# Causal attention with its score products in two row halves of the array, as 32-bit parts

## The reference

```
xn = layernorm(x)                                   # 4 sequences of 1024 tokens, 256 wide
Q, K, V = heads(xn @ W_q.T), heads(xn @ W_k.T), heads(xn @ W_v.T)     # 16 heads of 16
scores = Q @ K.T * 16 ** -0.5;  scores[k > q] = -inf
s = merge(softmax(scores) @ V) @ W_o.T
g = silu(two_layer_local_attention_network(xn))
out = x + s * g
```

## Time and profile before

| | |
|---|---|
| median of 3 runs | 2184.76 us (2183.27 to 2184.91) |
| profiled execution | 2185.67 us, span 2183.9 us |
| TensorE, busy | 1980.0 us (91%), weight loads 1414.1 us |
| VectorE, busy | 1559.4 us (71%) |
| ScalarE, busy | 1110.6 us (51%) |
| GpSimd, busy | 1072.4 us (49%) |
| mean granted clock of TensorE | 0.946 of 2.4 GHz |
| maxima products L517 | 768, 241.2 us busy |
| mask products L520 | 512 |
| maxima reductions L650 | 768, 375.9 us busy |
| score products L544 | 768, 191.8 us busy |
| weighted sums L562 | 1536 records (two for each of 768 products), 165.5 us busy |
| exponentials L627 | 384, 300.3 us busy |

### The profile page before, as it was taken

The page is one execution under the profiler, slowest core; times in us unless marked ns, Lnnn a source line. Parts: engine busy times, 40 slices in busy tenths (PEclk is TensorE's granted clock), DMA queues, the critical chain, the costliest instruction groups (busy, mean ns, idle before and its releaser), DMA issues. The chain is left out here.

```text
span 2183.9 us, 43787 instructions
## 1 busy us (share of the span) xinstructions
PE 1980.0 (91%) x13824; PEld 1414.1 (65%) x13888; DVE 1559.4 (71%) x2744; ACT 1110.6 (51%) x2339; POOL 1072.4 (49%) x903
## 2 busy tenths in 40 slices
PE   5869999999996899999997999779999999699976
PEld 4633334343432688888875888668888888578875
DVE  5657878778872799999995443269999999654324
ACT  3405656565665566666664222156666666422213
POOL 3431212112222666666663877476666666287730
PEclk9869999999998899999998999889999999799988
DMA  6892465464531000000022111200000002211137
GB/s 210 273 198 34 68 88 70 65 88 65 70 50 63 13 24 24 24 24 24 24 64 60 30 58 58 86 9 25 22 24 24 24 24 68 62 29 58 49 111 240
DMA packets 163938, 143.24 MB, mean 66 GB/s; under 512 B 30327, under 2 KB 144351, under 8 KB 163679
## 3 DMA queue, kind: packets, MB, share of 16 engines
q1 hardware_dynamic: 162462, 140.23, 27.4%
q10 hardware_dynamic: 1344, 1.31, 0.2%
HBM read 90.89 MB, written 50.35 MB: 65 GB/s over the span
## 5 line engine op out<-in xcount | busy, mean ns | idle before, releaser
L650 DVE TENSOR_REDUCE ca_mx<-ca_pR 128x1 f32<-128x512 f32 (+3 forms) x768 | 375.9, 549 | 91.0 <-PE ca_pR L520 47.8
L627 ACT ACTIVATE ca_pr<-ca_pS 128x1024 f32<-128x1024 f32 (+3 forms) x384 | 300.3, 813 | 244.2 <-PE ca_pS L544 185.0
L459 POOL TENSOR_SCALAR_AFFINE_SELECT ca_pr<-ca_pr 128x256 f32<-128x256 f32 x256 | 104.3, 408 | 430.3 <-ACT ca_pr L627 428.0
L879 ACT ACTIVATE w_pe<-w_pS,w_nmax 128x256 f32<-128x256 f32 x512 | 234.8, 484 | 142.3 <-DVE w_nmax L989 142.3
L802 POOL TENSOR_TENSOR w_tsn<-w_qk,w_tab 128x512 f32<-128x512 f32 x128 | 203.2, 1610 | 174.9 <-DVE w_pn L998 161.2
L517 PE MATMUL ca_pR<-ca_ks,ca_qs 96*128 96x512 bf16 (+3 forms) x768 | 241.2, 351 | 18.8 <-DVEq L703 16.2
L998 DVE TENSOR_SCALAR w_pn<-w_pe,w_rsum 128x256 f32<-128x256 f32 x512 | 227.3, 505 | 4.5
L544 PE MATMUL ca_pS<-ca_qs,ca_ks 98*128 98x512 bf16 (+3 forms) x768 | 191.8, 333 | 15.1 <-issue 13.2
L517 PEld LDWEIGHTS ca_pR<-ca_ks,ca_qs 96*128 96x128 bf16 x768 | 73.4, 99 | 186.5 <-DVE ca_mx L650 125.6
L810 POOL TENSOR_TENSOR w_rs<-w_ssc,mhalf 128x16 f32<-128x16 f32 x64 | 187.6, 2931 | 5.3
L1363 ACT ACTIVATE f_gl<-f_pH,f_b1g 128x512 f32<-128x512 f32 x96 | 66.2, 690 | 204.4 <-PE f_pH L1479 204.4
(11 more groups left out here) (163 smaller groups left out, 4777.3 us busy)
## 6 DMA issues: line engine op xcount, KB each, us to landing
QKP<-p_parts SPq DMA_DIRECT2D x32, 384.0 KB, 3.2
ca_qs<-QKP SPq DMA_DIRECT2D x96, 128.0 KB, 6.5
ca_ks<-QKP SPq DMA_DIRECT2D x96, 128.0 KB, 7.0
VA<-p_vaug SPq DMA_DIRECT2D x8, 1024.0 KB, 5.4
ca_va<-VA SPq DMA_DIRECT2D x16, 512.0 KB, 10.4
w_xt<-X SPq DMA_DIRECT2D x64, 128.0 KB, 2.0
X<-w_x SPq DMA_DIRECT2D x64, 128.0 KB, 1.7
f_hh<-X SPq DMA_DIRECT2D x32, 256.0 KB, 4.9
```

Of the source, the lines that this page charges most:

```text
L627: act.activation(pr[:, k % 2, pair, :, 0:w], pS[:, pair, :, 0:w], ACT.Exp, scale=CS).then_inc(p_ready, 1)
L650: dve.tensor_reduce(mx[:, i, h, ch:ch + 1], pR[jb % RING][:, 0:w], AX.X, ALU.max, negate=True).then_inc(ring_free, 1)
L879: ins = act.activation(pe_[:, h], pS[:, bank, slot], ACT.Exp, bias=nmax[:, n:n + 1], accum_out=sums[:, h:h + 1])
```

## The change

The queries and keys are kept as two 32-bit parts, high and low, where the high part is rounded to what a one-pass 32-bit product (`float32r`) takes. One ScalarE pass and one VectorE subtraction make them; the second ScalarE pass and GpSimd's subtraction go. A score needs three terms of 16 rows (high x high, high x low, low x high), 48 rows, and two more for the shift: 50. Two heads then lie in the two halves of the 128 rows, from partition 0 and from partition 64, and each half is multiplied by itself, into its own bank. The scores' two heads and the maxima's two heads are issued as such twos. A maxima pair waits for both of its banks before its first product, and the masks, still over 128 rows, follow both products. The jobs are reordered so that the two heads `r` of a pair `p` are neighbours, the plan of jobs per step changes to even numbers, the shift is placed by four transfers and the ones by six.

```diff
-PAIRS = [(0, 0), (0, 1), (0, 2), (1, 0), (1, 1), (2, 0)]
-SHIFT_ROW = len(PAIRS) * CD
-SROWS = SHIFT_ROW + 2
+TERMS = [(0, 0), (0, 1), (1, 0)]
+SHIFT_ROW = len(TERMS) * CD
+HALF_ROWS = 64
-LOADS = 2 * len(PAIRS) + 1
+LOADS = 2 * 2 * len(TERMS) + 1
...
-    parts = QKP[n].rearrange("(z h d) c s -> z c d h s", z=2, h=GH)
+    parts = QKP[n].rearrange("(z p r d) c s -> z c r d p s", z=2, p=2, r=2)
     out = []
-    for r, (a, k) in enumerate(PAIRS):
-        rows = slice(r * CD, (r + 1) * CD)
-        out += [(qs[rows, u], parts[0, a]), (ks[rows, u], parts[1, k])]
+    for r in range(2):
+        for t, (a, k) in enumerate(TERMS):
+            rows = slice(r * HALF_ROWS + t * CD, r * HALF_ROWS + (t + 1) * CD)
+            out += [(qs[rows, u].bitcast(F32), parts[0, a, r]), (ks[rows, u].bitcast(F32), parts[1, k, r])]
...
-        parts = sb("p1_parts", [P, CG, 3, SUP * P], BF16)
-        rest = sb("p1_rest", [P, CG, SUP * P], F32)
+        parts = sb("p1_parts", [P, CG, 2, SUP * P], F32R)
...
-                for g in range(CG):
-                    pool.wait_ge(part1, ONE + s * CG + g + 1)
-                    pool.tensor_tensor(parts[:, g, 2], rest[:, g], parts[:, g, 1],
-                                       ALU.subtract).then_inc(part2, 1)
...
-                    act.activation(parts[:, g, 0], pQ[:, g], ACT.Copy).then_inc(part0, 1)
-                    act.wait_ge(rest_ready, ONE + CG + u + 1)
-                    act.activation(parts[:, g, 1], rest[:, g], ACT.Copy).then_inc(part1, 1)
+                    act.activation(parts[:, g, 0], pQ[:, g], ACT.Copy).then_inc(part_hi, 1)
...
-                    dve.wait_ge(part0, ONE + u + 1)
-                    dve.wait_ge(part2, ONE + u + 1)
-                    dve.tensor_tensor(rest[:, g], pQ[:, g], parts[:, g, 0], ALU.subtract).then_inc(rest_ready, 1)
+                    dve.wait_ge(part_hi, ONE + u + 1)
+                    dve.tensor_tensor(parts[:, g, 1], pQ[:, g], parts[:, g, 0].bitcast(F32),
+                                      ALU.subtract).then_inc(part_lo, 1)
...
-    MAXJOBS = [(h, i, ch) for i in range(TPB - 1, -1, -1) for h in range(GH) for ch in range(1 + i // 4)]
+    MAXJOBS = [(p, r, i, ch) for i in range(TPB - 1, -1, -1) for p in range(2) for ch in range(1 + i // 4)
+               for r in range(2)]
-    PER = [6, 5, 4, 4, 5, 5, 5, 5, 2, 0, 0, 0]
-    EARLY = {10: (0, 3), 11: (3, 7)}
-    A, B = 2, 3
+    PER = [6, 4, 4, 4, 6, 6, 6, 4, 0, 0, 0, 0]
+    EARLY = {10: (0, 4), 11: (4, 8)}
+    A, B = 2, 4
...
-        shift = sb("ca_shift", [2 * GH, SEQ], BF16)
+        shift = sb("ca_shift", [2 * GH, SEQ], F32R)
+        one = sb("ca_one", [2, 2, SEQ], F32)
...
-            for u in range(SLOTS):
-                pool.memset(ks[SHIFT_ROW:SROWS, u, :, :], 1.0).then_inc(ones, 1)
-                pool.wait_ge(ones, ONE + u + 1)
+            pool.memset(one[:, :, :], 1.0).then_inc(made, 1)
...
                 for part in range(2):
-                    sp.dma_start(qs[SHIFT_ROW + part:SHIFT_ROW + part + 1, u, :, :],
-                                 shift[part * GH:(part + 1) * GH, :]).then_inc(shifted[u], 16)
+                    for r in range(2):
+                        row = r * HALF_ROWS + SHIFT_ROW + part
+                        sp.dma_start(qs[row:row + 1, u, :, :].bitcast(F32),
+                                     shift[part * GH + 2 * r:part * GH + 2 * r + 2, :].bitcast(F32)).then_inc(shifted[u], 16)
...
+                sp.wait_ge(made, ONE + 4)
+                for u in range(SLOTS):
+                    for r in range(2):
+                        row = r * HALF_ROWS + SHIFT_ROW
+                        sp.dma_start(ks[row:row + 2, u, :, :].bitcast(F32), one[:, :, :]).then_inc(ones, 16)
...
-                h, i, ch = MAXJOBS[idx]
-                k0 = ch * 512
-                w = min((i + 1) * P - k0, 512)
-                bank = ring(*job)
-                diag = k0 + w == (i + 1) * P
-                ins = pe.matmul(bank[:, 0:w], qs[0:SHIFT_ROW, u, h, i * P:(i + 1) * P],
-                                ks[0:SHIFT_ROW, u, h, k0:k0 + w], start=True, stop=not diag)
-                if diag:
-                    ins = pe.matmul(bank[:, w - P:w], K.identb[:, :], mask_q[:, :], start=False, stop=True)
-                ins.then_inc(ring_full, 1)
+                first, n_ring = job
+                banks = [ring(first + r, n_ring) for r in range(2)]
+                for r in range(2):
+                    p, half, i, ch = MAXJOBS[idx + r]
+                    rows = slice(r * HALF_ROWS, r * HALF_ROWS + SHIFT_ROW)
+                    k0 = ch * 512
+                    w = min((i + 1) * P - k0, 512)
+                    diag = k0 + w == (i + 1) * P
+                    ins = pe.matmul(banks[r][:, 0:w], qs[rows, u, p, i * P:(i + 1) * P], ks[rows, u, p, k0:k0 + w],
+                                    start=True, stop=not diag)
+                    if not diag:
+                        ins.then_inc(ring_full, 1)
+                for r in range(2):
+                    if diag:
+                        pe.matmul(banks[r][:, w - P:w], K.identb[:, :], mask_q[:, :], start=False, stop=True)\
+                          .then_inc(ring_full, 1)
...
-                for hh in range(2):
-                    h = pair * 2 + hh
-                    ins = pe.matmul(pS[:, pair, hh, 0:w], ks[:, u, h, j * P:(j + 1) * P],
-                                    qs[:, u, h, q0:q0 + w], start=True, stop=True)
+                for r in range(2):
+                    rows = slice(r * HALF_ROWS, r * HALF_ROWS + SHIFT_ROW + 2)
+                    ins = pe.matmul(pS[:, pair, r, 0:w], ks[rows, u, pair, j * P:(j + 1) * P],
+                                    qs[rows, u, pair, q0:q0 + w], start=True, stop=True)
```

More of the change, by code:

```diff
@@ L113, in phase_project @@
         t_ready, t_hi, t_lo = sem("p1_t_ready"), sem("p1_t_hi"), sem("p1_t_lo")
-        q_ready, part0, rest_ready, part1, part2 = (
-            sem("p1_q_ready"), sem("p1_part0"), sem("p1_rest_ready"), sem("p1_part1"), sem("p1_part2"))
+        q_ready, part_hi, part_lo = sem("p1_q_ready"), sem("p1_part_hi"), sem("p1_part_lo")
         part_stored = [sem(f"p1_part_stored{i}") for i in range(CG)]
@@ L148, in rest_of @@
                 for g in range(CG):
-                    sp.wait_ge(part2, ONE + CG + s * CG + g + 1)
+                    sp.wait_ge(part_lo, ONE + CG + s * CG + g + 1)
                     sp.dma_start(QKP[it * CG + g, :, :, j * 512:(j + 1) * 512],
-                                 parts[:, g]).then_inc(part_stored[g], 16)
+                                 parts[:, g].bitcast(F32)).then_inc(part_stored[g], 16)
                     if isinstance(s, int) and s == SUPERS - 2:
@@ L246, in _ @@
             start_at_one(dve, mine + K.stacks[3])
-            dve.sem_inc(rest_ready, CG)
+            dve.sem_inc(part_lo, CG)
             dve.sem_inc(v_copied, 2)
@@ L316, in step @@
                 for g in range(CG):
-                    pe.wait_ge(rest_ready, ONE + s * CG + g + 1)
+                    pe.wait_ge(part_lo, ONE + s * CG + g + 1)
                     ws = slice(g * P, (g + 1) * P)
@@ L574, in first @@
                 pe.wait_ge(loaded[0], ONE + LOADS * 16)
-                for idx in range(NJ):
+                for idx in range(0, NJ, 2):
                     maxima(idx, 0, 0, (idx, 0))
                 load_wait(1, 0)
-                for idx in range(NEARLY):
+                for idx in range(0, NEARLY, 2):
                     maxima(idx, 1, 1, (NJ + idx, 0))
@@ L586, in do @@
                     for job, kind, which in jobs:
+                        if kind in ("max", "early") and which % 2:
+                            continue
                         if kind == "max":
@@ L598, in step @@
                 if not started:
-                    pe.wait_ge(ones, ONE + SLOTS)
-                pe.wait_ge(shifted[u], ONE + (it + 1) * 2 * 16)
+                    pe.wait_ge(ones, ONE + SLOTS * 2 * 16)
+                pe.wait_ge(shifted[u], ONE + (it + 1) * 4 * 16)
                 for k in range(NSTEP):
@@ L645, in take_max @@
             def take_max(idx, job):
-                h, i, ch = MAXJOBS[idx]
+                p, r, i, ch = MAXJOBS[idx]
                 w = min((i + 1) * P - ch * 512, 512)
@@ L649, in take_max @@
                 dve.wait_ge(ring_full, ONE + n * RJ + jb + 1)
-                dve.tensor_reduce(mx[:, i, h, ch:ch + 1], pR[jb % RING][:, 0:w], AX.X, ALU.max,
+                dve.tensor_reduce(mx[:, i, 2 * r + p, ch:ch + 1], pR[jb % RING][:, 0:w], AX.X, ALU.max,
                                   negate=True).then_inc(ring_free, 1)
@@ L695, in step @@
                     elif kind == "shift":
-                        dve.wait_ge(shifted[u], ONE + (it + 1) * 2 * 16)
+                        dve.wait_ge(shifted[u], ONE + (it + 1) * 4 * 16)
                         take_shift((job, n))
@@ L1729, in program @@
         X = nc.dram_tensor("X", [(2 * LAYERS + 1) * ST_ROWS, D], F32, kind="Internal").ap()
```

(6 more changed lines are left out.)

1 line of the change is left out of this document (removed).

## The result

2375.51 us median (2357.55 to 2386.44, 4 runs) against 2184.84 us (2183.27 to 2186.38, 4 runs) before: a ratio of 1.086 [1.0804, 1.0917]. Forecast were 2229 us and a range up to 2290 us: slower was right, the size was not. The profiled execution took 2386.4 us where before took 2185.7, so the 200.7 us between these two have to be found. Three numbers of the timeline hold them: the first maxima product moved from 136.3 to 122.4 us (-13.9), from there to the first scores product it took 50.0 instead of 31.7 us (+18.3), and from the first to the last scores product, called the scores span from here on, 707.4 instead of 511.1 us (+196.3).

The account below looks back on a forecast made before the run. TensorE was taken to bind, VectorE close behind. Profiled 2185.7 us + 33 (15 iterations) + 11 (start of the block) = 2229.7, so a 2229 us median; own range 2205 to 2255, 8-in-10 range 2160 to 2290.

Parts of the forecast that it names:

- What binds, and the prices: Attention loop: TensorE binds with 29.4 us of work in 31.4, VectorE close behind; a 512-column pair in halves costs 0.23 us.
- rival 3: Scores and maxima: halves don't overlap for rounded 32-bit data, +8 us an iteration, 2315 us; chance 0.07.
- a masked pair: Maxima on the diagonal: a 512-column pair with masks and mode changes costs 0.70 us, where products and masks took 0.55.
- mode changes: Loop: TensorE's switches between row halves and full rows cost 8.4 us an iteration against 2.9 before, adding 5.5.
- rival 1: Loop: no drain between halves and mask, VectorE becomes the bound, 2168 us; chance 0.20 with every other way to a gain.
- The iteration: Loop, one head group: 33.6 us against 31.4 before, between 31.2 and 34.5; +33 us over 15 iterations.
- TensorE's own work: Loop, per iteration: products, masks, weighted sums, transposes and mode changes total 28.0 us against 29.4 before.
- The granted clock in the loop should stay near 1: Sign to check in the loop: TensorE's granted clock, 0.98 before, should stay near 1.
- rival 4: Loop: new waits drop the clock for a fifth of it, about +84 us more, 2290 to 2310 us; chance 0.10.
- The start of the block: First maxima before the first scores: 28 pairs worked out at 39.5 us against 27.1; +11 us taken, bounds 0 and +16.
- The projection: Before the attention block: splitting and moving the parts taken as 0, bounds -4 and +4 us.
- The shift's copy: Shift placement: 32-bit copy at most +1.4 us, four transfers +1.25; cost 0 in the loop, within +11 at the start.

Follow-up runs that it names:

- e13: Changed kernel with 14 more rows of zeros in each half (products of 62 and 64 rows): 2307.09 us, 1.0556 of before.
- e5: Kernel before (bf16, 96-row products, one-bank waits) with only the changed kernel's order and plan of jobs: 2204.98 us, 1.0092 of before.
- e4: Kernel before's bf16 96-row products with the changed kernel's order, plan and two-bank wait: 2272.6 us, 1.0392 of before.
- e11: Changed kernel with its two parts, stacks, shift and ones in bf16 instead of 32 bits (less exact): 2269.94 us, 1.0354 of before.
- e8: Changed kernel's 32-bit parts without halves, each head on full-array rows 0 to 66 (17 of zeros), in before's loop: 2438.35 us.
- e7: Changed kernel's 32-bit row halves, but each maxima product singly with its own half's mask and one bank, before's order and plan: 2283.07 us, 1.0437 of before.
- e15: e7 with the bf16 types of e11, leaving only the row halves of the loop's changes: 2199.8 us, 1.0049 of before.
- e1: Changed kernel with VectorE reducing only the last 128 columns of each maxima bank, so banks come free early: 2241.02 us, 1.0261 of before.
- e3: Changed kernel with every scores pair issued twice into the same banks: 2317.68 us, 1.0585 of before.
- the pairs in the table: Four pairs of kernels whose loops differ in rows of zeros alone: clock 0.66 to 0.81 with fewer rows, 0.85 to 0.95 with more.
- e12: Kernel before with the third part's subtraction done by VectorE instead of GpSimd: 2190.08 us, 1.0018 of before.
- e9: e8 with 48 rows of zeros instead of 17, so products take 96 or 98 rows: 2280.68 us, 1.0437 of before.
- e14: Kernel before's loop unchanged, projection making two bf16 parts instead of three, rows 64 to 95 zero (less exact): 2175.08 us, 0.9948 of before.

## Why the prediction was wrong

**What binds, and the prices: right.** TensorE binds; the halves overlap (0.24 us a pair, forecast 0.23; rival 3 falls); a masked pair costs 0.65 of the forecast 0.70, so the cost of the mode changes is real and rival 1 falls. The long weight load was seen as "no longer hidden", but priced at mode changes only.

**The iteration: too short by 2.3 us.** Forecast 33.6, between 31.2 and 34.5; the kernel after and e13 take 35.9 where the clock holds. Of the +4.5 us over before, the plan makes 1.05 (e5) and the two-bank wait 2.9 (e4): together 3.95, where the sum had 3.6 (from 2.0 us of waiting to 5.6). Mis-sized was the term "TensorE's own work", 28.0 against 29.4 us, so -1.4: row halves and 32-bit operands together cost 0.5 more instead (35.4 in e4, 35.9 after). In steps 4 to 11, where e11 held the clock, the halves save 1.0 us (23.3 to 22.3) and the 32-bit operands add 1.6 (22.3 to 23.9). The same operands cost 3.8 us an iteration in full rows (e8 against before) and about 2.1 in halves one by one (e7 against e15). These steps were taken in one order; in another order the shares could differ.

The start of the block shows one gap of the two-bank wait bare: pairs 122.36 to 124.00 = 1.64 us apart where 1.37 was forecast, since the first reduction starts 0.80 us after the pair, not 0.62 as after a single product, and the bank's next use comes 0.81 after that, not 0.75:

```profile
122.36 0.79 PE L518 MATMUL ca_pR<-ca_ks,ca_qs 48*128 48x512 f32 x2 [15.62 <-DVEq L709]
123.16 1.29 DVE L656 TENSOR_REDUCE ca_mx<-ca_pR 128x1 f32<-128x512 f32 x2 [13.71 <-PE ca_pR L518]
123.97 0.32 PEld L518 LDWEIGHTS ca_pR<-ca_ks,ca_qs 48*128 48x128 f32 x2 [1.32 <-DVE ca_mx L656]
124.00 0.79 PE L518 MATMUL ca_pR<-ca_ks,ca_qs 48*128 48x512 f32 x2 [0.84 <-DVE ca_mx L656]
```

**The step that failed: "The granted clock in the loop should stay near 1".** 15 iterations of +4.5 us make 67 of the 196 us in the scores span; the other 129 are what is left for the clock. It stood as rival 4, with a chance of 0.10 and "a fifth of the loop" at the low level, 2290 to 2310 us (its own sum, 2229 and 84, makes 2313). The loop's mean clock of 0.66 puts about two thirds of the time there. The forecast looked for the cause in waits alone, as at the start of the block. But e4 waits more and holds its clock, and e8 waits 29 us for reductions between 250 and 600 us, less than before's 77, and loses it. The change did three things that point one way: it cut the rows of a product from 96 and 98 to 48 and 50, made weight loads of 0.10 into 0.19 us, and thinned the stream by waits. The Trainium skill, "TensorE: Matmul & The Clock Gate", A second HAM failure mode: psum-queue depth-cycling, tells of a clock that swings because the engine idles briefly between groups while it cycles through banks. e1 agrees, e4 (0.94 with more waiting) doesn't, so here that rule alone doesn't decide. Each of e1 (waits), e11 (operands), e13 (rows) and e3 (more products) brings the clock part of the way back alone: 0.91, 0.78, 0.87 and 0.89 from 0.66.

**The low level lasts.** Before falls too: at some of its iterations' ends TensorE stands for 3.5 us without a wait that the profile shows, and the clock shows 0.57 and 0.58 in the two windows after 396 us and 1.00 in the next. In the kernel after it stays down for some 37 us at a busy share near 1, in e8 for over 100. That fewer rows hinder the return is what the pairs in the table suggest, and it isn't shown apart from an easier fall; the rule by which the chip decides was not measured and stays open.

**The start of the block:** +18.3 where +11 was forecast (bounds 0 to +16). The 28 pairs, from 122.36 us on, take 44.7 us where 39.5 was worked out (10 gaps of 1.64 off the diagonal, 18 of 1.2 to 1.9 on it), +5.2; 1.4 more had been taken off the worked-out +12.4 without a reason. VectorE shows only 9.47 of 14 us, against 13.07, so it doesn't bind there any more:

```profile
122.00:136.00 14.00, 7.46 (x26) 3.10 (x26) 9.47 (x16) 0.00 (x0) 0.94 (x1) 0.50 1.07 132
```

**The projection: 0 forecast with bounds of 4 us, -13.9 measured.** That TensorE's gap waits on the normalised input, "which none of this touches", was wrong: the period for four tiles fell from 13.2 to 10.8 us. e11, in bf16 with half the bytes, normalises at the same times (last one at 91.2 us in both, 103.4 before), so bytes aren't it. e12 moves GpSimd's pass to VectorE and gains nothing. By elimination, not by a run of its own, this leaves the chain of passes over a chunk (ScalarE, VectorE, ScalarE, GpSimd before, ScalarE, VectorE after), which the forecast priced at 0 since TensorE's wait named another releaser.

**The shift's copy** and its four transfers cost nothing in the loop that could be told apart, as forecast.

## What to carry to other kernels

Price a tiling change at both clock levels, and look at the rows its products take: fewer of them lowered the mean clock here even where columns and waits stayed the same. If a row group has free rows, try zeros in them; here 14 rows of zeros per half were worth 47 to 87 us of scores span; count what filling them costs ahead of the loop. Before changing an operand to 32 bits count the short products in front of its weight loads. And a wait for two banks of a ring of three leaves a ring of one and a half.

## What the hardware showed unexpectedly

- The granted clock rose with the rows that products take, zeros included (four pairs above). Issuing work twice made a kernel 58 us faster.
- VectorE's normalising took a mean of 607 ns per 256 columns with GpSimd's subtraction beside it, 475 in e12 and in the kernel after, where GpSimd has none:

```profile
L254 DVE TENSOR_SCALAR p_xn<-p_xin,p_mv,p_rstd 128x256 f32<-128x256 f32 x20 | 8.2, 475 | 5.1 <-POOL p_rstd L185 5.1
```

- The shift's copy of 8 x 1024 went from 679 ns (bf16 to bf16) to 1212 ns (bf16 to rounded 32-bit).
- Where the first maxima came at 122 us in the kernel after, filling zeros by transfers moved them to 160 us in e9 (48 rows of both stacks, three transfers each), to 185 us in e8 (17 rows, one transfer each) and to only 126 us in e13 (14 rows in each half). In e14 VectorE filled its rows in two times 5.18 us, which made the whole projection 10 us later.
